# Attention loop of a four-layer graph network: running sum of a tile's pieces added on PE, copied out by ACT

## The reference, cut to what matters

```python
q, k, v = jnp.split(qkv, 3, axis=-1)
scores = jnp.einsum('phi,phi->ph', q[src], k[dst]) / jnp.sqrt(jnp.float32(H))
m = jax.ops.segment_max(scores, src, num_segments=nV)
e = jnp.exp(scores - m[src])
denom = jax.ops.segment_sum(e, src, num_segments=nV)
w = e / denom[src]
att = jax.ops.segment_sum(w[:, :, None] * v[dst], src, num_segments=nV).reshape(nV, N * H)
```

## Time and profile before

| | |
|---|---|
| time, median of 3 runs | 8594.83 us (8592.99 to 8597.28) |
| profiled execution, first to last instruction (span) | 7455.3 us |
| outside the span, median of the runs less the span | 1139.5 us |
| busy in the span: PE / DVE / ACT / POOL | 5219.6 / 5497.7 / 2557.6 / 3747.2 us |
| attention loop | from about 5312 to about 6968 us of the span |
| mean granted TensorE clock of the span | 0.858 |

### The profile page before, as it was taken

One profiled execution on the slowest core, in us unless ns is written; L12 is line 12 of the kernel. 1 busy time (PEld: TensorE's weight loads), 2 busy tenths in 40 slices (PEclk: granted clock), 3 DMA queues, 4 the chain that ended last, 5 costly groups with the idle time before them and its releaser, 6 DMA issues.

```text
span 7455.3 us, 118434 instructions
## 1 busy us (share of the span) xinstructions
PE 5219.6 (70%) x23723; PEld 3771.2 (51%) x23723; DVE 5497.7 (74%) x13389; ACT 2557.6 (34%) x9063; POOL 3747.2 (50%) x3981
## 2 busy tenths in 40 slices
PE   0166666781766665787567777699777787787798
PEld 0144444450444443333256666588655565555687
DVE  8887777638888785775388998711499989898666
ACT  0033333220333231111146666411355555555211
POOL 0177777513777774333357777500355555555111
PEclk9877777795777777888789999999888888888899
DMA  0133333213333332001345555555555555555311
GB/s 12 38 101 102 101 102 102 84 51 101 102 101 107 111 101 83 31 30 35 98 130 157 157 156 156 149 161 161 157 157 162 163 154 159 157 157 156 74 44 36
DMA packets 421991, 818.61 MB, mean 110 GB/s; under 512 B 75256, under 2 KB 268648, under 8 KB 420842
## 3 DMA queue, kind: packets, MB, share of 16 engines
q0 software_dynamic: 194048, 574.45, 27.9%
q1 hardware_dynamic: 225002, 231.00, 9.9%
q10 hardware_dynamic: 2304, 6.29, 0.3%
HBM read 688.72 MB, written 269.09 MB: 128 GB/s over the span
## 4 chain that ended last, share of the span: by engine, by line
PE 29%; DVE 28%; POOL 16%; issue 15%; DMA 8%; ACT 2%; POOLq 1%; DVEq 1%; SPq 1%; ACTq 0%
POOL ring L716 12%; PE ps L1415 5%; DVE big L1350 5%; PE ps L797 4%; POOL big L1301 3%; DMA ring<-kv_d,gidx 3%; PE ps L1855 2%; PE ps L1872 2%; DVE big L338 2%; PE ps L1666 2%; DVE big L339 2%; DVE big L1759 2%; DVE big L1775 2%; DVE big L1340 2%; DMA ring<-x_d,idx 1%
## 5 line engine op out<-in xcount | busy, mean ns | idle before, releaser
L797 PE MATMUL ps<-ring 128*128 x3528 | 1471.8, 556 | 852.6 <-SPq L726 593.9
L797 PEld LDWEIGHTS ps<-ring 128*128 128x128 f32 x3528 | 728.4, 256 | 1283.9 <-issue 1225.3
L716 POOL DMA_INDIRECT ring<-in_x_dram,idx x832 | 833.0, 1001 | 578.6 <-DVEq L616 325.5
L778 ACT CAST ring<-ohb 128x128 f32<-128x128 bf16 x1764 | 523.4, 298 | 1685.9 <-DVE ohb L744 1662.8
L1537 POOL DMA_INDIRECT ring<-kv_d,gidx x754 | 712.9, 945 | 558.5 <-issue 518.6
L1301 POOL DMA_INDIRECT big<-x_d,idx x832 | 796.7, 958 | 349.9 <-issue 215.4
L716 POOL DMA_INDIRECT ring<-x_d,idx x832 | 831.2, 999 | 255.7 <-issue 240.0
L1365 PE MATMUL ps<-big,ring 128*128 128x128 f32 x4928 | 728.5, 291 | 303.3 <-DVE big L1340 163.1
L1365 PEld LDWEIGHTS ps<-big,ring 128*128 128x128 f32 x4928 | 621.1, 192 | 410.6 <-DVE big L1340 312.2
L754 DVE TENSOR_TENSOR big<-big,ps 128x257 f32 (+1 forms) x1764 | 752.7, 427 | 60.1 <-issue 29.0
L744 DVE TENSOR_SCALAR ohb<-iotab,keyf,nbase 128x128 bf16<-128x128 bf16 x1764 | 580.3, 329 | 235.6 <-PE ps L801 114.6
(11 more groups left out here) (370 smaller groups left out, 9293.4 us busy)
## 6 DMA issues: line engine op xcount, KB each, us to landing
bas_d<-big SPq DMA_DIRECT2D x1232, 128.0 KB
att_d<-wreg SPq DMA_DIRECT2D x464, 132.0 KB
big<-bas_d SPq DMA_DIRECT2D x49, 1024.0 KB, 5.6
x_d<-ring SPq DMA_DIRECT2D x147, 128.0 KB, 1.7
ring<-in_x_dram,idx POOLq DMA_INDIRECT x832
ring<-x_d,idx POOLq DMA_INDIRECT x832
big<-x_d,idx POOLq DMA_INDIRECT x832
kv_d<-ring SPq DMA_DIRECT2D x49, 260.0 KB, 2.3
```

Source lines behind the costliest of these rows:

```text
L716: nc.gpsimd.indirect_dma_start(out=rows[:, j, :], out_offset=None, in_=table, in_offset=bass.IndirectOffsetOnAxis(ap=idx_of(c), axis=0)).t ...
L778: S.copy(ohf[:, q % G1, :], ohb[:, q % G1, :]).then_inc(e["ohf"], 1)
L797: T.matmul(ps[k][:, 0:D], ohf[:, k, :], rows[:, slot, :].rearrange("p a d -> p (a d)"), start=True, stop=True)
```

## The change

The sum over a tile's pieces leaves DVE. PE adds the sum before by a third product into the same PSUM bank: the identity matrix times slot `kept * k` of a buffer `sums3` of ten slots. Slot 0 holds zeros, slots 1 to 8 the last eight sums, slot 9 the rescaled sum; `kept` is the table value (0 or 1) that DVE used as a per-pair factor before, now written into a table row and loaded into PE's registers. ACT copies the finished sum out of PSUM into its slot, as the first thing of its step, at lag 30. DVE's rescaling signals a new semaphore `accx`.

```diff
@@ tables of the sort by source
+            if s is by_src:
+                q.link(V.tensor_copy(to["tab"][96:97, 0:nq], to["keep"][96:97, 0:nq]))
@@ buffers
-        accx = ring[:, LOW * KVW + 512:LOW * KVW + 512 + AV]
+        sums3 = sb("sums3", [P, 10, AV])
+        acc, accx = sums3[:, 1:9, :], sums3[:, 9, :]
-        acc = wreg[:, 0:8 * AV].rearrange("p (s f) -> p s f", s=8)
-        LAG_U, LAG_ACC, LAG_PV, LAG_T = 22, 24, 26, 4
+        LAG_U, LAG_OUT, LAG_PV, LAG_T = 22, 30, 26, 4
@@ l3_edges_act, first in step
+                if live(c, LAG_OUT, N3):
+                    u = (c - LAG_OUT) // 2
+                    act.wait_ge(l3["pv"], u + 1)
+                    if u >= 8:
+                        act.wait_ge(flushed[u % 8], 16 * (NCH // 8 + u // 8))
+                    S.copy(acc[:, u % 8, :], ps[3 + u % 2][:, 0:AV]).then_inc(l3["acc"], 1)
                 if live(c, LAG_T, N3):
@@ l3_edges_pe, last in step
+                    if (j - LAG_PV) % GRP == 0:
+                        kept[:] = load_group(mybir.EngineType.PE, pend_i, c - LAG_PV, GRP, 1)
                     for a in range(2):
-                        last = T.matmul(ps[3 + t][:, 0:AV], oh3[:, jj + a, :], weighted[:, t, a * AV:(a + 1) * AV], start=(a == 0), stop=(a == 1))
-                    last.then_inc(l3["pv"], 1)
+                        T.matmul(ps[3 + t][:, 0:AV], oh3[:, jj + a, :], weighted[:, t, a * AV:(a + 1) * AV], start=(a == 0), stop=False)
+                    if u % 8:
+                        pe.wait_ge(l3["acc"], u)
+                    else:
+                        pe.wait_ge(l3["accx"], u // 8 + 1)
+                    T.matmul(ps[3 + t][:, 0:AV], ident[:, :],
+                             sums3[:, bass.ds(kept[(j - LAG_PV) % GRP] * (u % 8 or 9), 1), :].rearrange("p a f -> p (a f)"),
+                             start=False, stop=True).then_inc(l3["pv"], 1)
@@ l3_edges_dve
-            q.link(V.memset(acc[:, :, :], 0.0))
+            q.link(V.memset(sums3[:, :, :], 0.0))
-                    q.link(V.tensor_tensor(accx..., acc[:, 7]..., ps[6]..., ALU.mult))
+                    V.tensor_tensor(accx..., acc[:, 7]..., ps[6]..., ALU.mult).then_inc(l3["accx"], 1)
-            def add(c, j, i):
-                ...
-                V.scalar_tensor_tensor(out=acc[:, k], in0=before, scalar=keep[:, bass.ds(c - LAG_ACC, 1)], in1=ps[3 + u % 2][:, 0:AV],
-                                       op0=ALU.mult, op1=ALU.add).then_inc(l3["acc"], 1)
-                if live(c, LAG_ACC, N3):
-                    add(c, j, i)
```

More of the change, by code:

```diff
@@ L1514, in by_head @@
             return row.rearrange("p (m n) -> p m n", m=HEADS)
-        l3 = {k: sem(f"l3_{k}") for k in ("oht", "q", "prod", "s", "u", "pv", "acc")}
+        l3 = {k: sem(f"l3_{k}") for k in ("oht", "q", "prod", "s", "u", "pv", "acc", "accx")}
         b3 = {"pk": n1["tr"], "gk": n1["hT"], "st": n1["mm"], "ends": n1["rz"], "rows": n1["pre"], "car": n1["y"],
@@ L1601, in step @@
                     S.activation(crow, argrow, ACT.Exp, scale=SCALE).then_inc(b3["cr"], 1)
-            walk(act, N3, R3, 12, step, flat=True)
+            walk(act, N3, R3, LAG_OUT, step, flat=True)
         def l3_edges_pe(pe):
@@ L1608, in l3_edges_pe @@
             at = [None] * GRP
+            kept = [None] * GRP
             def step(c, j, i):
@@ L1731, in chain @@
                         dve.wait_ge(l3["acc"], B3 // 2 * b)
-                    q.link(V.tensor_tensor(accx.rearrange("p (m e) -> p m e", m=HEADS),
-                                           acc[:, 7].rearrange("p (m e) -> p m e", m=HEADS),
-                                           ps[6][:, 0:HEADS].unsqueeze(2).broadcast_to([P, HEADS, HD + 1]), ALU.mult))
-            def add(c, j, i):
-                u, jj = (c - LAG_ACC) // 2, j - LAG_ACC
-                k = u % 8
-                dve.wait_ge(l3["pv"], u + 1)
-                if past(u, 8):
-                    dve.wait_ge(flushed[k], 16 * (NCH // 8 + u // 8))
-                if k:
-                    dve.wait_ge(l3["acc"], u)
-                    before = acc[:, k - 1]
-                else:
-                    before = accx
-                V.scalar_tensor_tensor(out=acc[:, k], in0=before, scalar=keep[:, bass.ds(c - LAG_ACC, 1)], in1=ps[3 + u % 2][:, 0:AV],
-                                       op0=ALU.mult, op1=ALU.add).then_inc(l3["acc"], 1)
+                    V.tensor_tensor(accx.rearrange("p (m e) -> p m e", m=HEADS),
+                                    acc[:, 7].rearrange("p (m e) -> p m e", m=HEADS),
+                                    ps[6][:, 0:HEADS].unsqueeze(2).broadcast_to([P, HEADS, HD + 1]), ALU.mult).then_inc(l3["accx"], 1)
             def step(c, j, i):
@@ L1785, in step @@
                                     AX_X, ALU.add).then_inc(l3["s"], 1)
-            walk(dve, N3, R3, LAG_ACC, step, flat=True)
+            walk(dve, N3, R3, LAG_U, step, flat=True)
         LINKS_B = 15
```

## The result

The changed kernel takes 8923.7 us (median of 4, 8909.23 to 8929.14) against 8593.91 us before (8587.31 to 8597.28): ratio 1.0388, interval 1.0374 to 1.0403, **330 us slower**. The forecast was 9050 us.

A forecast was written before the change was run, and what follows sets the result against it. DVE, 90% busy, was taken to bound the attention loop. A batch going from 27.8 to 35.6 us, times 58, gave +452; small edits made it +457 on 8594.83: forecast 9050 us, range 8880 to 9250.

The forecast's parts named there:

- Which engine's order decides: Attention loop: ACT's copy-out waits for PE's step end, PE's next step for ACT; they alternate, 4.06 us a pair against 2.20.
- The hand-over: ACT's part of the closed loop: two releases, the new copy and the two instructions behind it, 1.19 us a pair.
- The first: Rival: the hand-over does not close the loop, PE becomes the bound, DVE's relief wins: -128 us, 8467 us; 7%.
- the third rival: Without a closed loop, longer plain pairs and shorter chain pairs cancel: -0.1 us a batch, -6 us, 8589 us; 3%.
- The signs that were named: New profile: L1784 about 4.4 us apart, PE waiting some 500 us for ACT, DVE some 60% busy, POOL's and DMA's waits gone.
- PE's part: PE's share of the closed loop, from weight load through the identity product (0.45): 2.72 us a pair at full clock.
- the fourth rival: The register address makes PE drain before each identity product: 0.7 us a pair, +325 us on top, 9375 us; 3%.
- The sequencer: Table loads on PE's sequencer, partly covered by running products: 0.15 us a pair taken, between nothing and 0.33.
- The batch's extras: Batch chain: PE's other work in order, plus waits for `u` (0.75) and `accx` (0.2): 3.15 us a batch.
- PE's clock in the plain pairs: Full clock assumed in the loop, because third-layer edges with similar bursts and rests were granted 1.00.
- the second rival: PE gets half clock half of the time, as in the first layer (0.77): +561 us, 9610 us; 6%.
- The base: Starting point: 27.8 us a batch from the profile, with 1139.5 us around the span left as they are.

The follow-up runs named there:

- e3: Kernel before plus only a wait for PE's products and a dummy copy first in ACT's step; DVE still adds: 8711.32 us, ratio 1.0141, on the slower chip.
- e2: Changed kernel without PE's identity product, its table load and its wait; copy-out still first in ACT's step: 8708.23 us, ratio 1.0129, on the slower chip.
- e9: Changed kernel with ACT's copy-out moved from first to last in its step, on the quicker chip: 7460.53 us, ratio 0.9997.
- e1: Changed kernel with ACT's copy-out moved from first to last in its step, on the slower chip: 8776.38 us, ratio 1.021.

## Why the forecast was right in sign and off in size

**Which engine's order decides: right.** The step on which the prediction stood, that the copy-out waits for the last product of a PE step and holds back the two instructions that PE's next step needs, is shown three ways. The hand-over costs by itself, with DVE's and PE's work as before (e3, +118 us on A, although the late signals of before are gone from it). DVE's relief is worth nothing under it (e2 equals e3). And moving the copy-out takes all of the cost away (e9). How the cost divides is less sure: e3's 34.2 us a batch is 2.1 above before on A, which has its late signals, and would be 6.4 of the 9.6 us above before on B if it held there, where it was not run. The first and the third rival fell with it for the change as it is. With the loop open (e9) the third came true in its total, and the first, which had the same condition and promised -128 us, did not: 7 us were gained, within the noise.

**The hand-over: right.** 1.19 us predicted, 1.15 measured. The releases of 0.03 and 0.08 were 0.04 and 0.05, and the copies start 0.27 apart. The signs that were named are there too, though DVE's reductions start 4.7 us apart and not 4.4: PE waits in 394 of the stretch's 424 pairs, 453 us in 2000 (some 500 in the loop were expected), DVE's busy share is 58%, and its wait for the gathers (33.0 us from 5400 to 6900 before) is gone.

**PE's part: right.** 2.72 us predicted, 2.67 measured, of which the identity product holds 0.61 to its end (0.45 predicted, from a start-to-start distance, with the tail counted in L1666's 1.05). No gap stands before it but the one for `accx`, so the fourth rival fell. The 0.4 us "of pipeline" in its price stands in no row; what the trace shows of that kind is the 0.16 us by which the product's end (0.61) lies behind the time for which it holds PE (0.45).

**The sequencer: mis-sized.** 0.15 us a pair were taken between bounds of 0 and 0.33. Every other pair is longer by 4.38 - 3.82 = 0.56: 0.28 a pair. The plain pair is 4.10 us on average against 4.06, since the small excess of the two terms above cancels this. The reasoning failed too: the old load does not hide behind a running product, because after a hand-over nothing is running but the short L1628. The new load does hide, but a load takes 0.50 us in this loop, not the 0.33 of the earlier trace rows.

**The batch's extras: mis-sized, with one cause missing.** 3.15 us were taken; 37.43 - 8 x 4.10 = 4.6 were measured. The waits themselves came out near: 0.92 for `u` (0.75 predicted) and 0.41 for `accx` (0.2). What was missing is the clock behind them. At 0.96 on average over this loop, 8% of a batch, 3.0 us, is at the lower level, and half of that, 1.5 us, is lost, which agrees with the 1.4 us counted above. The stretch that gives the 0.96, after on B:

```profile
5500.00:7400.00 1900.00, 1306.86 (x5584) 910.98 (x5585) 1106.60 (x2559) 919.56 (x3727) 761.61 (x805) 0.96 0.43 117
```

**PE's clock in the plain pairs: right.** The twin chosen from the third layer holds: 1.15 us of rest in each 3.8 to 4.4 us, granted clock 1.00; the second rival (0.77, +561 us) fell. The Trainium skill, page TensorE: Matmul & The Clock Gate, section "A second HAM failure mode: psum-queue depth-cycling", says that short frequent rests make the clock swing between its levels; the plain pairs of this trace do not agree with it. The clock does fall to 0.50 and 0.53 at L1677, but there a thinly filled stretch or very small products came first, and it happens about once a batch and not from pair to pair.

**The base: wrong.** This is the step that failed by most. The prediction took 27.8 us a batch from the profile and put 1139.5 us "around the span", left as they are. They were inside the span of the timed chip, and 4.2 us of each batch were among them. The loop that the change slows had late signals there, and under the new one they are gone. By the numbers: +452 from 35.6 - 27.8; less 4.24 x 58 = 246 for the base; plus (37.77 - 35.6) x 58 = 126 for the batch that was too short: +332, and 330 was measured. The two errors have opposite signs; had the chip been B, +457 would have stood against +577, and the forecast would have been 120 us too low. That 8923.7 lies inside 8880 to 9250 is thus in part luck: with a batch as long as predicted, 35.6 us, the changed kernel would have taken about 8594 + (35.6 - 32.1) x 58 = 8797 us on A, under the range, and only the batch that was too short in the sum brought it back in.

A difference of 1139.5 us between span and runs, 13% of the time, was itself a sign. A constant around the span was one reading of it, and a profile of a quicker execution was the other; the prediction weighed only the first.

## What to carry to other kernels

Moving work from the busiest engine to another is priced by where the moved work waits, not by how long it runs: here 0.40 us less on DVE and 0.27 more on ACT in a pair cost 577 us at the head of a step and nothing at its end. Ask what stands behind a new wait in that engine's queue, and whether the engine it waits for needs that very thing next; if so the two alternate, and the pair costs the sum of both. A wait on the last thing of another engine's step belongs at the end of one's own.

## What the runs showed of the hardware that was not expected

- The same program takes 7467 us on two of the chips and 8594 us on the third. On the third, engines go on microseconds after the last thing they waited for at certain places (277.8 us in 56 waits of L1568), and the stages before the attention loop are longer too (L1365: 1497 instead of 1021 us, at a granted clock of 0.77 instead of 0.99). The cause stays open: the runs meant to test the gathers for it fell on the other kind of chip.
- The ratio of two kernels can differ by chip, 1.0388 and 1.0787 for this change: before is 4.2 us a batch longer on A than on B, the changed kernel 0.3. The late signals are in before and e1 on A and not in the closed loops of after, e2 and e3; why these are spared was not tested.
- A load of four table values on PE's sequencer took 331 ns by the median in a loop with four of them a batch and 504 ns in one with eight, and after a hand-over its whole duration lay on PE's path (0.32 and 0.49 us). Why it grew was not looked into.
- TensorE was granted 2.4 GHz through regular rests of 1.15 us between 2.7 us of products, and 1.2 GHz for one group of products after a rest of 0.92 us that followed a thinly filled step.
